# Cross attention on one core: the row sums of a group directly behind its product with v, and its normalisation a step sooner

## The reference

```python
q_c = _ln(x) @ W_qc + b_qc
kv_c = _ln(context) @ W_kvc + b_kvc
k_c, v_c = jnp.split(kv_c, 2, axis=-1)
...
c_attn_w = jax.nn.softmax(jnp.einsum('bhqd,bhsd->bhqs', q_c, k_c) * scale, axis=-1)
c_attn_out = jnp.einsum('bhqs,bhsd->bhqd', c_attn_w, v_c)
```

## Time and profile before

| | |
|---|---|
| median of 3 runs | 2788.36 us (2788.08 to 2788.68) |
| profiled execution | 2788.28 us |
| its span (first to last instruction) | 2786.2 us |
| mean granted clock of TensorE | 0.974 of full speed |
| PE busy | 2675.9 us, 96% of the span |
| DVE busy | 1741.9 us, 63% |
| ACT busy | 1118.2 us, 40% |
| POOL busy | 1299.6 us, 47% |
| 16 DMA engines | q1 34.3% of their span, q0 0.8% |
| row maxima, DVE L1470 | 512 x 927 ns |
| POOL L1635, L1637, L1639 | 252 x 1154, 1161 and 675 ns |

### The profile page before, as it was taken

One profiled execution on the slowest core, in us unless ns is written; L12 is line 12 of the kernel. 1 busy time (PEld: TensorE's weight loads), 2 busy tenths in 40 slices (PEclk: granted clock), 3 DMA queues, 4 the chain that ended last, 5 costly groups with the idle time before them and its releaser, 6 DMA issues. The chain is left out here.

```text
span 2786.2 us, 49955 instructions
## 1 busy us (share of the span) xinstructions
PE 2675.9 (96%) x18608; PEld 2142.2 (77%) x18608; DVE 1741.9 (63%) x3285; ACT 1118.2 (40%) x2187; POOL 1299.6 (47%) x1447
## 2 busy tenths in 40 slices
PE   7999999999889999999999999999869999999997
PEld 5688888888577787777777877777558888888886
DVE  5677777777736777777777766776744444444431
ACT  3344444444434554455545555554532212212110
POOL 1445445454414767766766676676810220220211
PEclk9999999999789999999999999999779999999999
DMA  8454544545342434443344344333431111111110
GB/s 238 107 127 109 127 126 124 131 111 151 96 125 79 110 104 107 108 116 106 103 116 112 105 109 115 107 82 95 128 109 33 41 53 35 39 49 35 42 42 23
DMA packets 169359, 269.86 MB, mean 97 GB/s; under 512 B 28928, under 2 KB 83200, under 8 KB 169104
## 3 DMA queue, kind: packets, MB, share of 16 engines
q1 hardware_dynamic: 166048, 259.33, 34.3%
q0 software_dynamic: 3072, 7.34, 0.8%
HBM read 111.11 MB, written 36.77 MB: 53 GB/s over the span
## 5 line engine op out<-in xcount | busy, mean ns | idle before, releaser
L1470 DVE TENSOR_REDUCE cross_nmax<-cross_sc_ps 112x1 f32<-112x750 f32 x512 | 459.2, 927 | 157.9 <-PE cross_sc_ps L1345 157.8
L1588 ACT ACTIVATE cross_prT<-cross_tr_ps 125x448 f32<-125x448 f32 x768 | 389.9, 544 | 152.9 <-PE cross_tr_ps L1364 145.2
L1635 POOL TENSOR_TENSOR cross_part<-cross_prT 125x448 f32<-125x448 f32 x252 | 290.8, 1154 | 149.0 <-PE cross_or_ps L1384 83.3
L997 POOL TENSOR_TENSOR self_psum<-self_prT 112x224 f32<-112x224 f32 x256 | 175.9, 687 | 367.1 <-ACT self_prT L889 199.6
L1364 PE MATMUL cross_tr_ps<-cross_qst,cross_kst 98*125 98x224 f32 x1536 | 313.0, 290 | 7.7 <-ACT cross_prT L1588 3.9
L1364 PEld LDWEIGHTS cross_tr_ps<-cross_qst,cross_kst 98*125 98x125 f32 x1536 | 243.4, 189 | 91.7 <-ACT cross_prT L1588 39.2
L1637 POOL TENSOR_TENSOR cross_part<-cross_part,cross_prT 125x448 f32<-125x448 f32 x252 | 292.7, 1161 | 19.8
L2030 ACT ACTIVATE mlp_hv<-mlp_h_ps,mlp_b 128x512 f32<-128x512 f32 x112 | 77.1, 689 | 522.0 <-PE mlp_h_ps L73 507.9
L1345 PE MATMUL cross_sc_ps<-cross_kst,cross_qst 96*112 96x500 f32 (+1 forms) x1024 | 272.6, 348 | 7.1 <-DVE cross_nmax L1470 3.9
L1947 DVE CAST mlp_hT_h<-mlp_hv 128x512 fp32r<-128x512 f32 x112 | 51.0, 455 | 323.3 <-ACT mlp_hv L2030 323.3
L889 ACT ACTIVATE self_prT<-self_st_ps 112x448 f32<-112x448 f32 x256 | 139.1, 544 | 216.2 <-PE self_st_ps L469 216.2
(11 more groups left out here) (241 smaller groups left out, 6634.6 us busy)
## 6 DMA issues: line engine op xcount, KB each, us to landing
cross_kst<-cross_nat_h SPq DMA_DIRECT2D x512, 93.8 KB, 2.2
cross_c_in<-in_context SPq DMA_DIRECT2D x96, 250.0 KB
cross_kst<-cross_nat_l SPq DMA_DIRECT2D x256, 93.8 KB, 2.2
cross_qst<-qc SPq DMA_DIRECT2D x192, 112.0 KB, 2.4
self_kst<-self_nat_h SPq DMA_DIRECT2D x128, 112.0 KB, 2.3
self_qst<-self_natq_h SPq DMA_DIRECT2D x128, 112.0 KB, 2.9
self_x_in<-in_x SPq DMA_DIRECT2D x16, 448.0 KB, 3.8
self_kst<-self_nat_l SPq DMA_DIRECT2D x64, 112.0 KB, 2.3
```

What stands on the lines that cost most here:

```text
L997: pool.tensor_tensor(psum[:, j], prT[:, j, 0], prT[:, j, 1], ALU.add).then_inc(p_summed, 1)
L1470: dve.tensor_reduce(nmax[:, g % 2, t, j:j + 1], sc_ps[t][0:QN, SC0:SC0 + S], AX_X, ALU.max, negate=True).then_inc(maxed, 1)
L1588: act.activation(prT[:, slot(h), 2 * c:2 * c + 2], bank((h + LAG) % NH, c)[0:SN, 0:2 * N].rearrange("p (k t) -> p k t", k=2), ACT.Exp).the ...
L1635: pool.tensor_tensor(part[:], prT[:, j, 0:2], prT[:, j, 2:4], ALU.add).then_inc(pre_summed, 1)
```

## The change

Three loops move; nothing is computed in another way. PE makes the sums of a group in the step of its product with v, right behind it (for all groups but the last). DVE inverts one step after the product in place of two, and normalises two steps after it in place of three. POOL stores two steps after it in place of three, ahead of its sum of that step's head.

```diff
@@ -1411,8 +1411,7 @@
                         pv(o, g)
                         if whole(o, g * HPG):
                             whole_sums(g)
-                    for o, g in late_group(b, h - 1, att, prv):
-                        if not whole(o, g * HPG):
+                        else:
                             sums(o, g)
                     for f, o in fill_at(b, h, "c"):
                         fill_(o, f)
@@ -1512,9 +1511,9 @@
-                    for o, g in late_group(b, h - 2, att, prv):
+                    for o, g in late_group(b, h - 1, att, prv):
                         invert(o, g)
-                    for o, g in late_group(b, h - 3, att, prv):
+                    for o, g in late_group(b, h - 2, att, prv):
                         normalize(o, g)
```

More of the change, by code:

```diff
@@ L1514, in body @@
                         low(o, f)
+                    for o, g in late_group(b, h - 1, att, prv):
+                        invert(o, g)
                     for o, g in late_group(b, h - 2, att, prv):
-                        invert(o, g)
-                    for o, g in late_group(b, h - 3, att, prv):
                         normalize(o, g)
```

## The result

| | before | changed |
|---|---|---|
| median, runs side by side | 2788.52 us (2788.08 to 2790.15, 4 runs) | 2812.61 us (2812.26 to 2813.6, 4 runs) |
| ratio | | 1.0084, 95% interval 1.0072 to 1.0095 |
| profiled execution, span | 2788.28, 2786.2 us | 2812.26, 2810.3 us |
| mean granted clock | 0.974 | 0.972 |

The change makes the kernel 24 us slower. The forecast was 2813. By the page of the changed kernel, PE is busy 1.2 us longer in a span that is 24 us longer, so taken over the whole run the time is idle time of PE. (The last stretches of the cross phase are another matter, see the bullet on the end.)

The account below looks back on a forecast made before the run. PE was taken to set the time of the cross attention phase and POOL that of its end. 14 x 0.63 + 13 x 0.78 = +19 us, +6 at the end, on 2788.3 gave 2813 us; range 2794 to 2827.

Parts of the forecast that it names:

- The sums in the stream: Eight more records directly behind each product with v cost PE 0.36 us, four times per period of sixteen steps.
- What comes back at the old place: PE time regained where sums stood: 0.55 us in steps 11 and 15, 0.60 in step 7, nothing in step 3.
- 14-2: Stretch from PE's product with v in step 14 to that in step 2; forecast -0.19 us a period.
- 10-14: Stretch from PE's product with v in step 10 to that in step 14; forecast +0.52 us a period.
- 2-6: Stretch from PE's product with v in step 2 to that in step 6; forecast +0.78 us a period.
- 6-10: Stretch from PE's product with v in step 6 to that in step 10; forecast +0.30 us a period.
- The normalisation ahead of the low part of k: On DVE in step 4: k's low part, PE's next projection and step 6's product come 0.37 us later.
- The wait of step 6: PE's sums behind step 6's product wait 0.61 us for POOL's sums of the group's last head; net +0.54.
- The wait of step 10: PE's sums behind step 10's product wait 0.78 us on POOL, DVE's mean instruction being held up; net +0.71.
- Step 2, +0.05, step 14, none: PE's waits on POOL's sums after these products: +0.05 us taken in step 2, no wait in step 14.
- The end: Last stretches, POOL-bound: 0.9 us for each of four groups, +2 at the very end; together +6, bounds 0 and 10.
- The rivals: Waits don't come: 2789 or 2784 us, chance 0.14. Waits cost the clock in the periods: 2844, chance 0.06.

Follow-up runs that it names:

- D3: B1 with each of PE's sums steps made twice, 16 records in place of 8, into the same place; 2813.25 us, ratio 1.0085.
- C1: Kernel before with sums directly behind the product, store in its old step but behind that step's head; 2786.67 us, ratio 0.9991; again 2786.82.
- A2: Kernel before with only reciprocal, normalisation and store a step sooner, sums at their old place; 2796.24 us, ratio 1.0022.
- B1: Changed kernel with POOL's store behind its sum of that step's head in place of ahead of it; 2791.54 us, ratio 1.0006.
- B2: Changed kernel with DVE's small instruction for the mean ahead of the reciprocal in its step; 2806.86 us, ratio 1.0059.
- D2: C1 with PE's sums one step behind the product in the last batch alone; 2784.25 us, ratio 0.9981.
- C2: Kernel before with only the store moved behind POOL's sum of that step's head; 2789.67 us, ratio 1.0001.
- C3: C1 with one reciprocal, that of step 4, moved to step 5; 2792.3 us, ratio 1.0012.

## Why the prediction was right, point by point

- **The sums in the stream, 0.36 each.** Right: 0.36 to 0.40 in D3.
- **What comes back at the old place, 0.55 / 0.55 / 0.60 / 0.** 14-2 is -0.19, as worked out. In 10-14 and 2-6, read from C1 (-0.19 and +0.36), 0.55 and 0 too. Only 6-10 was mis-sized: -0.33 without waits, so 0.70 came back and not 0.60. The other 0.10 lies one instruction further on, past the point to which the prediction read. The transposed scores of the next step take 1459.33 - 1459.01 = 0.32 to the next start behind the sums (before), and 1459.58 - 1459.37 = 0.21 without them (C1):

```profile
1459.01 0.48 PE L1364 MATMUL cross_tr_ps<-cross_qst,cross_kst 98*125 98x224 f32 x2
1459.33 0.40 PE L71 MATMUL cross_pj_ps<-cross_wkv_l,cross_cT_h 128*125 128x512 f32 x1
```

```profile
1459.37 0.38 PE L1364 MATMUL cross_tr_ps<-cross_qst,cross_kst 98*125 98x224 f32 x2
1459.58 0.40 PE L71 MATMUL cross_pj_ps<-cross_wkv_l,cross_cT_h 128*125 128x512 f32 x1
```

- **The normalisation ahead of the low part of k, 0.37.** 0.30 (A2, and B1 less C1: 0.66 - 0.36). I took the instruction's duration; the next one starts 1460.00 - 1459.70 = 0.30 after it, since the duration overlaps its neighbour. The distance of the starts was the right figure.
- **The wait of step 6, 0.61, net 0.54.** Sums without a wait start 2.29 behind the product and not 2.18, so 0.49 late; the time lost is 0.52 (B1). The 7.29 us from normalisation to POOL's sum were 7.28.
- **The wait of step 10, 0.78, net 0.71.** 0.73 by B1. Adding up the prediction's own terms gives the POOL sums at 1473.96 and not 1473.98, which changes nothing. The share of the instruction that POOL holds up was worked out as 0.36; B2 gave back 0.42, which can also have a part from the other place of the instruction.
- **Step 2, +0.05, step 14, none.** No wait in either: POOL's sums are ready 0.11 us ahead of PE's need in step 2 and 2.2 us in step 14. In 2-6, 0.66 for 0.78, this 0.05 and the 0.07 above are all of the difference.
- **The end, +6.** The number came out (+6.1), but by luck, since it is not made up as forecast. The stretches are +0.5, +2.3, +2.4, +2.9, -0.3, -1.7, where 0.9 for each of four and 2 at the very end were worked out from POOL's time. Over these six stretches, before and then changed, with the same 561 matmuls:

```profile
1938.49:2022.08 83.59, 70.57 (x561) 44.97 (x560) 58.93 (x82) 43.96 (x89) 68.77 (x68) 0.82 0.42 119
1956.76:2046.42 89.66, 75.87 (x561) 48.79 (x560) 59.01 (x82) 43.57 (x89) 66.61 (x66) 0.76 0.40 109
```

  PE is busy 5.3 us longer at a granted clock of 0.76 for 0.82, and idle only 0.8 longer. POOL, which was taken to set the pace there, stands idle for 23.1 us in place of 14.8. So most of the +6 is matmuls that run slower, not waits at the sums. Whether PE's waits brought the clock down is not shown. The experiments don't divide the 6.1 either. B1 (2.7 less than the changed kernel), C1 (2.5 less than B1) and D2 (2.5 less than C1) end 1.6 below before, and these are single executions: C1's two agree to 0.1, but B1's was the slowest of its ten, 2.9 above their median.
- **The rivals.** The waits came. In the periods the clock cost nothing: from the first product to the last batches it is 1.00 in both traces, where PE is busy 6.6 us less in 16.8 us more. At the end it was lower, as the bullet above shows; the prediction had this rival in the periods only. Over the run it is 0.972 against 0.974.
- **The sum.** 2813 for 2812.61 is better than the terms deserve. They made 19 us in the periods and 6 at the end. The trace has 16.8 and 6.1, and the 1.5 us ahead of the phase, which no term covers, fill most of the gap. The prediction also counted 14 stretches 10-14 and 13 stretches 2-6, where the table has 15 and 14. That did little harm: the last of each are only +0.23 and +0.33.

The largest single claim, that POOL's store stood in the way and not POOL's work, was only argued in the prediction; B1 shows it, and C2 shows that the same move does nothing where PE asks for the sums a step later.

## What to carry to other kernels

When a consumer is moved a step sooner, look at what stands in the producer's queue ahead of its input: here it was not the producer's 3.1 us of work but a DMA issue that waited 2.94 us for a third engine. Put such a store behind the work that others wait for. A change that turns slack into an earlier start should move only the instructions that profit: the sums, with the store behind POOL's head, were worth 2 to 6 us, while the sooner reciprocal and normalisation cost some 4 (B1's 1.0006 against C1's 0.9991), and where an engine runs out of filler, as in the last batch, the old order is the better one.

## What the runs showed of the hardware that I had not expected

- The exclusion between DVE and POOL isn't a fixed cost. Of two instructions that start within 0.02 us of one another, DVE's lasted 0.17 us in 5 batches and 1.15 in 9 (C3), and a difference of some ns in the start goes with it. An edit elsewhere that shifts two engines against one another can switch it on or off: C3 lost 7.5 us by it, more than it was meant to gain over C1, and in B1 the instruction for the mean fell from 0.93 to 0.13 us though only a store had moved.
- An idle time in brackets counts from the modelled end of the instruction before. For 32-column matmuls that flow into one another it understates the delay: 0.30 shown for 0.49 late, 0.54 for 0.73.
